# Eight masked copies of the messages per edge type, or seven and a difference weight

## The chip, the cores and the metric

The kernel runs on one core of one Trainium2 chip. The metric is the device time of one launch in microseconds (us), as the median of the runs.

## The reference, cut to what matters

Two layers of a relational graph network over 50,000 nodes and 50,000 edges, 128 features, 8 edge types. Each edge makes a message from its source row; the message is multiplied by the 128x128 weight of its type, divided by the number of edges of that type at its destination, and added up there.

```
m = jax.nn.relu(h[src] + xe)                     # one message an edge
seg = etype * n + dst
sums = jax.ops.segment_sum(m, seg, num_segments=R * n)
mean = sums / jnp.maximum(cnt, 1.0)[:, None]
out = jnp.einsum('rnd,rdo->no', mean.reshape(R, n, -1), w)   # R = 8 weights
out = out + h @ rt + b
h = _batch_norm(out, gamma, beta)                # then relu, in layer 0
```

Before layer 0 every row goes through a layer norm and relu, and at the end the input x is added.

## The kernel before

**Stages.** About 174 us of preparation (indices turned, edge counts, first 56 row gathers), then for each layer an edge loop and a node loop. The edge loop of layer 0 lies at about 174 to 1180 us of the span, its node loop at 1180 to 1525; the edge loop of layer 1 at 1524 to 2582, its node loop to 2825; then the output pass.

**Edge loop.** The edges are cut into tiles of 127 (one row is kept for a carried partial sum), 394 tiles a layer, four tiles a group (`H = 4`), so 99 groups a layer. A group is 128 partitions by 512 values. Its steps, each engine working through its own list in order:

- POOL (GpSimd) gathers four times 128 rows by index (line 468) 14 groups ahead and scatters four times 128 result rows (line 476) of the group itself. In the loop it issues them by turns: gather, scatter, gather, scatter (lines 507 to 512). The first scatter of a group waits for `ob_ready`, the first gather for the transposes of the group that held its buffer.
- DVE (VectorE) goes through this order (lines 736 to 747): layer-norm statistics of group i+3 (`group_stats`, layer 0 only), the masked copies of group i (`by_type`, line 719), scales of group i+3 (`group_scales`, layer 0 only, waits for ACT's square root), edge sum of group i+2 (`edge_sum`: line 703 in layer 0, lines 706, 707 and 709 in layer 1), and the matrix that joins equal destinations, of group i (`same_node`, line 732, waits for PE's `keys`).
- `by_type` makes eight copies of the messages `mt`, copy r being zero where the edge's type, read from PSUM, isn't r. It waits for PE to have finished the products two groups back (`mk` has two slots).
- PE (TensorE) multiplies, for each tile, the eight copies by the eight weights into one sum (`products`, line 1069), and then joins equal destinations (`node_sums`, line 1086). Transposes of group i+2 (`turn`, line 1039) stand behind the second tile's products of group i.
- ACT (ScalarE) writes `mt` (`message`, line 859), copies the products out (line 867), carries the last row from tile to tile (line 879) and copies the sums to `ob` (line 887), which has four slots and waits for the scatter that used the slot to land.

**Preparation's end.** PE turns the inverse counts (line 995), DVE copies them (lines 669 and 670) and goes straight into the loop. PE waits for all parameters (`params_in`, line 1031) before it. The weights of both layers lie in SBUF from the start (`w_sb`, loaded at line 832).

Of the kernel before, what the change touches and what calls it, by code (L numbers as in the profile page):

```python
# [6 lines left out]
P = 128  # L7
# [4 lines left out]
ALU = mybir.AluOpType  # L12
ACT = mybir.ActivationFunctionType
# [4 lines left out]
def wait(eng, sem, value):  # L18

    if value > 0:  # L20
        eng.wait_ge(sem, value)
# [20 lines left out]
def gnn_kernel(nc, x, src, dst, edge_attr, edge_type, weight, root, bias, gamma, beta, out):  # L42
    N, D = x.shape
    E = src.shape[0]
    L, R = weight.shape[0], weight.shape[1]
# [19 lines left out]
    W4 = H * D  # L65
# [16 lines left out]
    def tiles(g):  # L82
        return range(g * H, min(g * H + H, NT))

    ctx = ExitStack()
    with ctx:
# [3 lines left out]
        def sem(name):  # L90
            return ctx.enter_context(nc.semaphore(name))
# [14 lines left out]
        def part(which, mem, shape, dt=FP32):  # L106
            n = math.prod(shape[1:])
            flat = mem[:, used[which]:used[which] + n]
            used[which] += n
            if dt != FP32:  # L110
                flat = flat.bitcast(dt)
            if len(shape) == 3:
                flat = flat.rearrange("p (a b) -> p a b", a=shape[1])
            if len(shape) == 4:
                flat = flat.rearrange("p (a b c) -> p a b c", a=shape[1], b=shape[2])
            return flat

        def early(shape, dt=FP32):
            return part("arena", arena, shape, dt)
# [9 lines left out]
        w_sb = [early([P, R * D]) for l in range(L)]  # L129
# [65 lines left out]

        hb = early([P, HB, H, D])
        xb = early([P, XB, H, D])
        mt = early([P, 2, W4])

        rows_b = early([P, NB * P])[:, :].bitcast(BF16).rearrange("p (k b e) -> p k b e", k=2, b=NB)  # L200
        ident_b = early([P, P // 2])[:, :].bitcast(BF16)
        mk = mk_mem.rearrange("p (s r n) -> p s r n", s=2, r=R)
# [25 lines left out]
        def pb(name):  # L228
            return ctx.enter_context(nc.psum_tensor(name, [P, W4], FP32))

        ps_t = [pb("ps_t0"), pb("ps_t1")]
        ps_y = [pb("ps_y0"), pb("ps_y1")]
        ps_o = [pb("ps_o0"), pb("ps_o1")]
        ps_s = [pb("ps_s0"), pb("ps_s1")]
        ps_turn, ps_key, ps_type = ps_t[0], ps_t[1], ps_s
# [8 lines left out]
        params_in = sem("params_in")  # L244
# [25 lines left out]
        inv_out = sem("inv_out")  # L270
        tminv_in = sem("tminv_in")
        inv_ps = sem("inv_ps")
        got = [sem(f"got{s}") for s in range(HB)]
        xb_in = [sem(f"xb_in{s}") for s in range(XB)]
        scat_out = [sem(f"scat_out{s}") for s in range(OB)]
# [5 lines left out]
        m_ready = sem("m_ready")  # L281
        tr_ps = sem("tr_ps")
        mk_ready = sem("mk_ready")
        s_ready = sem("s_ready")
        y_ps = sem("y_ps")
# [246 lines left out]
        def _(dve):  # L532
            v = nc.vector
# [135 lines left out]
            own.link(v.tensor_copy(inv_t[:, :], ps_y[0][:, :]))  # L669
            own.link(v.memset(inv_t[0:1, :], 1.0))  # L670

            def flat(ap):
                return ap.rearrange("p c d -> p (c d)")

# [20 lines left out]
            def edge_sum(g, l):  # L695
                gg = l * NG + g
                w = len(tiles(g))
                h4 = hb[:, gg % HB, 0:w, :]
                x4 = xb[:, gg % XB, 0:w, :]
                if l == 0:  # L700
                    dve.wait_ge(h_ready, g + 1)
                    dve.wait_ge(xb_in[gg % XB], xb_count(gg))
                    v.tensor_tensor(flat(h4), flat(h4), flat(x4), ALU.add).then_inc(t_ready, 1)
                else:
                    dve.wait_ge(got[gg % HB], 16 * tiles_done(gg, HB))
                    own.link(v.tensor_tensor(h4, h4, bn_b[:, 0, :].unsqueeze(1).to_broadcast([P, w, D]), ALU.mult))
                    own.link(v.tensor_tensor(h4, h4, bn_b[:, 1, :].unsqueeze(1).to_broadcast([P, w, D]), ALU.add))
                    dve.wait_ge(xb_in[gg % XB], xb_count(gg))
                    v.scalar_tensor_tensor(flat(h4), flat(h4), 0.0, flat(x4), ALU.max, ALU.add).then_inc(t_ready, 1)

            def by_type(g, l):

                gg = l * NG + g
                n = len(tiles(g)) * D
                dve.wait_ge(types_ps, gg + 1)
                dve.wait_ge(m_ready, gg + 1)
                wait(dve, y_ps, gg - 1)
                for r in range(R):
                    ins = v.scalar_tensor_tensor(mk[:, gg % 2, r, 0:n], ps_type[gg % 2][:, 0:n], float(r), mt[:, gg % 2, 0:n],  # L719
                                                 ALU.is_equal, ALU.mult)  # L720
                ins.then_inc(mk_ready, 1)

# [13 lines left out]
            for l in range(L):  # L736
                for i in range(-3, NG):
                    if l == 0 and i + 3 < NG:
                        group_stats(i + 3)
                    if i >= 0:  # L740
                        by_type(i, l)
                    if l == 0 and i + 3 < NG:
                        group_scales(i + 3)
                    if 0 <= i + 2 < NG:
                        edge_sum(i + 2, l)
                    if i >= 0:
                        same_node(i, l)
# [18 lines left out]
                def add_own(c, l=l):  # L766
                    s = c % SLOTS
                    cc = l * NC + c
                    dve.wait_ge(ac_in[s], 16 * (l * chunk_uses(NC - 1 - (NC - 1 - s) % SLOTS) + chunk_uses(c)))
                    for q in range(2):  # L770
                        dve.wait_ge(own_ps, 2 * cc + q + 1)
                        rows = flat(ac[:, s, q * H:q * H + H, :])
                        v.tensor_tensor(rows, rows, ps_o[q][:, :], ALU.add).then_inc(sum_ready, 1)  # L773
# [47 lines left out]
        def _(act):  # L821
            a_ = nc.scalar
# [13 lines left out]
            n = (KEYS + P) // P  # L836
# [17 lines left out]
            def message(g, l):  # L854
                gg = l * NG + g
                n = len(tiles(g)) * D
                act.wait_ge(tr_ps, gg + 1)
                wait(act, mk_ready, gg - 1)
                a_.activation(mt[:, gg % 2, 0:n], ps_turn[:, 0:n], ACT.Relu).then_inc(m_ready, 1)  # L859

            def products_out(g, l):
                gg = l * NG + g
# [27 lines left out]
            for l in range(L):  # L890
                for i in range(-3, NG + 2):
                    if 0 <= i - 2:
                        carry(i - 2, 0, l)
                    if 0 <= i + 1 < NG:
                        message(i + 1, l)
                    if 0 <= i - 2:
                        carry(i - 2, 1, l)
                    if l == 0 and i + 3 < NG:
                        root_of(i + 3)
                    if 0 <= i - 2:  # L900
                        carry(i - 2, 2, l)
                    if 0 <= i - 1 < NG:
                        products_out(i - 1, l)
                    if 0 <= i - 2:
                        carry(i - 2, 3, l)
                        sums_out(i - 2, l)
                    if l == 0 and i + 3 < NG:
                        normalised(i + 3)
# [77 lines left out]
        def _(pe):  # L986
            te = nc.tensor

            def on_all(to, col):

                return te.matmul(to, col.to_broadcast([P, P]), ident[:, :], start=True, stop=True)
# [16 lines left out]
            for w in range(2):  # L1008
                te.matmul(ps_y[1][0:R, w * P:(w + 1) * P], tails[:, w, :], ident[:, :], start=True, stop=True)
                last = te.matmul(ps_y[1][0:R, (2 + w) * P:(3 + w) * P], through[:, w:w + 1].to_broadcast([P, R]), ident[:, :],  # L1010
                                 start=True, stop=True)
            last.then_inc(rows_ps, 1)
            pe.wait_ge(carries_ready, 1)
            for w in range(2):
                last = te.matmul(ps_s[1][:, w * R:(w + 1) * R], row_carry[:, w, w:w + P], ident[0:R, 0:R], start=True, stop=True)
# [14 lines left out]
            cols(ps_y[0], tm_inv).then_inc(inv_ps, 1)  # L1030
            pe.wait_ge(params_in, 16 * 5 * L)
            pe.wait_ge(meta_ready, 1)

            def turn(g, l):
                gg = l * NG + g
                pe.wait_ge(t_ready, gg + 1)
                wait(pe, m_ready, gg)
                for j in range(len(tiles(g))):
                    last = te.transpose(ps_turn[:, j * D:(j + 1) * D], hb[:, gg % HB, j, :], ident[:, :])  # L1039
                last.then_inc(tr_ps, 1)  # L1040
# [19 lines left out]
            def products(g, j, l):  # L1060
                gg = l * NG + g
                if j >= len(tiles(g)):
                    return
                c = slice(j * D, (j + 1) * D)
                if j == 0:
                    pe.wait_ge(mk_ready, gg + 1)
                    wait(pe, yb_ready, gg - 1)
                for r in range(R):
                    last = te.matmul(ps_y[gg % 2][:, c], mk[:, gg % 2, r, c], w_sb[l][:, r * D:(r + 1) * D],  # L1069
                                     start=r == 0, stop=r == R - 1)  # L1070
                if j == len(tiles(g)) - 1:
                    last.then_inc(y_ps, 1)

# [14 lines left out]
            for l in range(L):  # L1088
# [57 lines left out]
                if l == 0:  # L1146
                    pe.wait_ge(bn_ready, 1)
                    for k in range(2):
                        last = on_all(ps_o[0][:, k * D:(k + 1) * D], bn_col[:, 0, k:k + 1])
# [3 lines left out]
            for c in range(NC):  # L1153
                k = c - KEPT
                sums = kept[:, c, :] if k < 0 else spare[:, k % 2, :]
                for q in range(2):
                    pe.wait_ge(aff_ready, 2 * c + q + 1)
                    wait(pe, f_ready, 2 * (c - 1) + q + 1)
                    for j in range(H):
                        a = (q * H + j) * D  # L1160
                        last = te.transpose(ps_t[q][:, j * D:(j + 1) * D], sums[:, a:a + D], ident[:, :])  # L1161
# [24 lines left out]
```

## Time and profile before

| | us |
|---|---|
| median of 3 runs | 3026.44 |
| lowest and highest run | 2994.49, 3029.53 |
| profiled execution, its time | 3015.93 |
| its span, first to last instruction | 3014.1 |

The profile's page gives the busy time of each engine over the span, the span in 40 slices, and the chain of work that ended last. All instants below are us from the start of the span. An engine that is busy for most of the span need not set the end: one has to read, stage by stage, which wait ends last. "Issue" is time before an instruction in which its engine waited for nothing that the profile shows.

### The profile page before, as it was taken

To read this page: it belongs to the slowest core of one execution; us is meant where nothing else is said; L and a number is where in the kernel's file an instruction comes from. 1 tells how busy PE (TensorE), PEld (TensorE's weight loads), DVE (VectorE), ACT (ScalarE), POOL (GpSimd) and SP (SyncE) were. 2 spreads that over 40 slices of the span, in tenths; PEclk is the share of its full clock that TensorE was granted. 3 is DMA by queue.
4 is the path that set the end of the run, shared out by engine and by line. 5 is a ranking of instruction groups with operands and counts; after the bars stand their busy time and mean duration, and the time that the engine had idled before them with its cause. 6 is when DMAs were issued, how large, how long until landed. Compare 5 with 4: busy or idle time off the path is not lost.

```text
span 3014.1 us, 55442 instructions
## 1 busy us (share of the span) xinstructions
PE 2356.7 (78%) x20114; PEld 2261.9 (75%) x20114; DVE 2183.5 (72%) x5449; ACT 1088.4 (36%) x2709; POOL 1590.4 (53%) x1586
## 2 busy tenths in 40 slices
PE   0059999999888896767678888888988889787553
PEld 0059998888888896656678888888888889677443
DVE  2789988788878885777787777777777778365432
ACT  0024444343443443656622222222222222455443
POOL 5117777777777773000057777777777776100000
PEclk9999999999999998988889999999999999899755
DMA  9222232323222223666732122222222221567799
GB/s 371 80 91 94 85 100 87 101 94 103 92 92 97 70 62 88 231 224 224 240 113 57 55 58 61 62 65 68 68 66 67 68 69 43 185 240 270 261 318 310
DMA packets 224768, 386.65 MB, mean 128 GB/s; under 512 B 39743, under 2 KB 148046, under 8 KB 224492
## 3 DMA queue, kind: packets, MB, share of 16 engines
q1 hardware_dynamic: 149494, 214.88, 22.6%
q0 software_dynamic: 50432, 80.31, 8.8%
q10 hardware_dynamic: 24566, 87.86, 7.5%
q8 instruction: 164, 2.69, 0.4%
q14 instruction: 112, 0.92, 0.1%
HBM read 241.77 MB, written 164.19 MB: 135 GB/s over the span
## 4 chain that ended last, share of the span: by engine, by line
POOL 44%; PE 17%; issue 14%; DMA 13%; DVE 6%; another core or an unknown queue 2%; ACT 1%; SPq 1%; POOLq 1%; ACTq 0%; DVEq 0%
POOL acc L476 22%; POOL arena L468 22%; PE ps_y L1069 7%; DMA chunk_mem<-in_x_dram 5%; PE ps_o L1120 4%; DMA chunk_mem<-h_rows 4%; DMA out_dram<-chunk_mem 2%; PE ps_s L1134 2%; DMA spare<-spill 2%; DVE st L753 1%; PE ps_t L1110 1%; DVE chunk_mem L601 1%; PE ps_o L1086 1%; POOLq L476 1%
## 5 line engine op out<-in xcount | busy, mean ns | idle before, releaser
L1069 PE MATMUL ps_y<-arena 128*128 128x128 f32 x12608 | 1553.5, 277 | 7.9 <-DVE arena L719 7.9
L1069 PEld LDWEIGHTS ps_y<-arena 128*128 128x128 f32 x12608 | 1487.8, 194 | 8.4 <-DVE arena L719 8.4
L719 DVE SCALAR_TENSOR_TENSOR arena<-ps_s,arena 128x512 f32<-128x512 f32 x1584 | 960.4, 677 | 71.9 <-PE ps_y L1069 71.9
L476 POOL DMA_INDIRECT acc<-arena x788 | 810.6, 1029 | 296.6 <-issue 236.1
L468 POOL DMA_INDIRECT arena<-h_rows,arena x394 | 393.8, 1000 | 463.6 <-DMA h_rows<-chunk_mem 343.9
L468 POOL DMA_INDIRECT arena<-in_x_dram,arena x394 | 384.5, 976 | 229.8 <-issue 119.3
L1086 PE MATMUL ps_o<-arena 128*128 128x128 f32 x1576 | 332.0, 292 | 187.9 <-ACT arena L879 187.2
L732 DVE TENSOR_SCALAR arena<-ps_t,arena 128x128 f32<-128x128 f32 x788 | 269.1, 403 | 206.6 <-PE ps_t L1046 206.6
L1086 PEld LDWEIGHTS ps_o<-arena 128*128 128x128 f32 x1576 | 239.5, 192 | 222.5 <-ACT arena L879 221.2
L879 ACT ACTIVATE arena<-ps_o 1x128 f32<-1x128 f32 x786 | 205.3, 261 | 439.4 <-PE ps_o L1086 407.7
L887 ACT ACTIVATE arena<-ps_o 128x512 f32<-128x512 f32 x198 | 116.5, 589 | 508.6 <-DMA acc<-arena 506.0
L1120 PE MATMUL ps_o<-root_sb,ht 128*128 128x128 f32 x1568 | 228.3, 307 | 79.0 <-ACT ht L917 78.3
L1120 PEld LDWEIGHTS ps_o<-root_sb,ht 128*128 128x128 f32 x1568 | 213.8, 219 | 91.0 <-ACT ht L917 91.0
L867 ACT ACTIVATE arena<-ps_y 128x512 f32<-128x512 f32 x198 | 117.7, 595 | 302.4 <-PE ps_y L1069 300.9
L773 DVE TENSOR_TENSOR chunk_mem<-chunk_mem,ps_o 128x512 f32<-128x512 f32 x196 | 130.6, 685 | 88.9 <-PE ps_o L1120 81.5
L1110 PE MATMUL ps_t<-ident,chunk_mem 128*128 128x128 f32 x784 | 112.1, 289 | 92.3 <-DMA chunk_mem<-h_rows 52.2
L1110 PEld LDWEIGHTS ps_t<-ident,chunk_mem 128*128 128x128 f32 x784 | 90.3, 147 | 110.1 <-DMA chunk_mem<-h_rows 62.6
L851 ACT ACTIVATE arena<-arena,nmr,rstd 128x128 f32<-128x128 f32 x394 | 161.2, 481 | 6.0 <-DVE nmr L692 6.0
L927 ACT ACTIVATE chunk_mem<-chunk_mem,nmr,rstd 128x128 f32<-128x128 f32 x392 | 156.0, 482 | 10.6 <-DVE nmr L764 10.2
L859 ACT ACTIVATE arena<-ps_t 128x512 f32<-128x512 f32 x198 | 114.2, 577 | 108.3 <-PE ps_t L1039 107.7
L753 DVE BATCH_NORM_STATS2 st<-chunk_mem 128x6 f32<-128x128 f32 x392 | 80.5, 278 | 96.9 <-DMA chunk_mem<-in_x_dram 96.6
L818 DVE TENSOR_TENSOR chunk_mem<-chunk_mem,ps_t 128x512 f32<-128x512 f32 x98 | 65.1, 685 | 117.1 <-PE ps_t L1161 57.9
(135 smaller groups left out, 1882.9 us busy)
## 6 DMA issues: line engine op xcount, KB each, us to landing
chunk_mem<-acc SPq DMA_DIRECT2D x98, 512.0 KB, 4.1
arena<-in_edge_attr_dram SPq DMA_DIRECT2D x194, 256.0 KB
chunk_mem<-in_x_dram SPq DMA_DIRECT2D x98, 448.0 KB, 4.8
acc<-arena ACTq DMA_DIRECT2D x28, 896.0 KB, 26.3
acc<-arena SPq DMA_DIRECT2D x28, 896.0 KB
h_rows<-chunk_mem ACTq DMA_DIRECT2D x49, 512.0 KB, 4.1
chunk_mem<-h_rows SPq DMA_DIRECT2D x49, 512.0 KB, 4.7
out_dram<-chunk_mem ACTq DMA_DIRECT2D x49, 448.0 KB, 4.6
```

Source lines behind the costliest of these rows:

```text
L468: pool.indirect_dma_start(out=hb[:, gg % HB, t - g * H, :], out_offset=None, in_=(x, h1_tab)[l], in_offset=at(src_t[:, t:t + 1])).then_inc ...
L476: pool.indirect_dma_start(out=acc[l], out_offset=at(idx_t[:, t:t + 1]), in_=ob[:, gg % OB, t - g * H, :], in_offset=None, bounds_check=N - ...
L719: ins = v.scalar_tensor_tensor(mk[:, gg % 2, r, 0:n], ps_type[gg % 2][:, 0:n], float(r), mt[:, gg % 2, 0:n], ALU.is_equal, ALU.mult)
L732: ins = v.tensor_scalar(sm[:, gg % SM, c], ps_key[:, c], ikey_t[:, t:t + 1], inv_t[:, t:t + 1], ALU.is_equal, ALU.mult)
L773: v.tensor_tensor(rows, rows, ps_o[q][:, :], ALU.add).then_inc(sum_ready, 1)
L851: ins = a_.activation(row, row, ACT.Relu, scale=rstd[:, g % 2, j:j + 1], bias=nmr[:, g % 2, j:j + 1])
L879: a_.activation(yb[0:1, n % 2, (t + 1) % H, :], ps_o[gg % 2][0:1, j * D:(j + 1) * D], ACT.Copy).then_inc(carried, 1)
L927: ins = a_.activation(row, row, ACT.Relu, scale=rstd[:, c % 2, j:j + 1], bias=nmr[:, c % 2, j:j + 1])
L1069: last = te.matmul(ps_y[gg % 2][:, c], mk[:, gg % 2, r, c], w_sb[l][:, r * D:(r + 1) * D], start=r == 0, stop=r == R - 1)
L1086: te.matmul(ps_o[gg % 2][:, c], sm[:, gg % SM, c], yb[:, gg % 2, j, :], start=True, stop=True).then_inc(o_ps, 1)
L1110: last = te.transpose(ps_t[j // H][:, (j % H) * D:(j % H + 1) * D], xc[:, s, j, :], ident[:, :])
L1120: last = te.matmul(ps_o[q][:, j * D:(j + 1) * D], ht[:, c % 2, k:k + D], root_sb[:, l * D:(l + 1) * D], start=True, stop=True)
```

## The change

Instead of eight masked copies, seven are made (types 0 to 6). The eighth product of each tile multiplies the unmasked messages `mt` by the last type's weight, and the weights of the other seven types are replaced once, on DVE before the loop, by their difference to the last one. Since PE now reads `mt` itself, `mt` gets a third slot, and ACT waits before it writes a slot for the products of three groups back instead of for the masks of two groups back. PE waits once for the differences.

```diff
-        mt = early([P, 2, W4])
+        mt = early([P, 3, W4])
...
+            dve.wait_ge(params_in, 16 * 5 * L)
+            for l in range(L):
+                ws = w_sb[l][:, 0:(R - 1) * D].rearrange("p (r o) -> p r o", o=D)
+                ins = v.tensor_tensor(ws, ws, w_sb[l][:, (R - 1) * D:R * D].unsqueeze(1).to_broadcast([P, R - 1, D]), ALU.subtract)
+            ins.then_inc(w_ready, 1)
...
-                for r in range(R):
-                    ins = v.scalar_tensor_tensor(mk[:, gg % 2, r, 0:n], ps_type[gg % 2][:, 0:n], float(r), mt[:, gg % 2, 0:n],
+                for r in range(R - 1):
+                    ins = v.scalar_tensor_tensor(mk[:, gg % 2, r, 0:n], ps_type[gg % 2][:, 0:n], float(r), mt[:, gg % 3, 0:n],
                                                  ALU.is_equal, ALU.mult)
...
-                wait(act, mk_ready, gg - 1)
-                a_.activation(mt[:, gg % 2, 0:n], ps_turn[:, 0:n], ACT.Relu).then_inc(m_ready, 1)
+                wait(act, y_ps, gg - 2)
+                a_.activation(mt[:, gg % 3, 0:n], ps_turn[:, 0:n], ACT.Relu).then_inc(m_ready, 1)
...
             pe.wait_ge(meta_ready, 1)
+            pe.wait_ge(w_ready, 1)
...
-                for r in range(R):
-                    last = te.matmul(ps_y[gg % 2][:, c], mk[:, gg % 2, r, c], w_sb[l][:, r * D:(r + 1) * D],
-                                     start=r == 0, stop=r == R - 1)
+                for r in range(R - 1):
+                    te.matmul(ps_y[gg % 2][:, c], mk[:, gg % 2, r, c], w_sb[l][:, r * D:(r + 1) * D], start=r == 0, stop=False)
+                last = te.matmul(ps_y[gg % 2][:, c], mt[:, gg % 3, c], w_sb[l][:, (R - 1) * D:R * D], start=False, stop=True)
```

## Rows read from the trace of the kernel before

**Rows 1.** The page: busy time, share of span and instructions; then the chain by engine.
```profile
PE 2356.7 (78%) x20114; PEld 2261.9 (75%) x20114; DVE 2183.5 (72%) x5449; ACT 1088.4 (36%) x2709; POOL 1590.4 (53%) x1586
...
POOL 44%; PE 17%; issue 14%; DMA 13%; DVE 6%; another core or an unknown queue 2%; ACT 1%; SPq 1%; POOLq 1%; ACTq 0%; DVEq 0%
```

**Rows 2.** POOL's groups, 210 to 1085, then 1640 to 2490: busy, mean ns | idle before.
```profile
L476 POOL DMA_INDIRECT acc<-arena x335 | 341.9, 1021 | 129.2 <-issue 100.9 <-ACT arena L887 28.3
L468 POOL DMA_INDIRECT arena<-in_x_dram,arena x335 | 328.5, 981 | 102.2 <-issue 101.9 <-ACT arena L887 0.3
...
L476 POOL DMA_INDIRECT acc<-arena x321 | 335.8, 1046 | 97.8 <-issue 97.8
```

**Rows 3.** Lines 468 and 476, 210 to 1085, then 1600 to 2490: ns min/median/max.
```profile
L468 POOL DMA_INDIRECT arena<-in_x_dram,arena x335: 973/973/1450, 212.0 to 1084.1; - x168
...
L476 POOL DMA_INDIRECT acc<-arena x335: 1014/1014/1534, 210.7 to 1082.8; - x168
...
L468 POOL DMA_INDIRECT arena<-h_rows,arena x336: 969/973/1447, 1600.7 to 2489.4; - x168
...
L476 POOL DMA_INDIRECT acc<-arena x336: 1012/1012/1487, 1599.4 to 2488.0; - x168
```

**Rows 4.** Busy time in two stretches: us, PE, PEld, DVE, ACT, POOL, PEclk, DMA, GB/s.
```profile
210.00:1085.00 875.00, 804.29 (x7303) 788.19 (x7303) 735.41 (x2088) 366.74 (x1043) 670.28 (x670) 0.99 0.29 92
...
1600.00:2490.00 890.00, 778.06 (x7007) 756.86 (x7005) 685.96 (x1252) 217.06 (x581) 685.55 (x672) 0.99 0.21 63
```

**Rows 5.** The chain that ended last, in order of time: start, us, what.
```profile
1085.43 2.21 DMA acc<-arena
...
1101.82 1.79 PE ps_y L1069 x16
...
1110.80 1.79 PE ps_y L1069 x16
```

**Rows 6.** DVE's waits, 210 to 1085, then 1640 to 2490: total, times, longest.
```profile
DVE rstd L691 <- ACT sd L845: 76.1, 55, 2.7
DVE arena L732 <- PE ps_t L1046: 52.7, 85, 2.3
...
DVE arena L732 <- PE ps_t L1046: 127.5, 76, 4.3
DVE arena L719 <- PE ps_y L1069: 58.9, 80, 1.2
```

**Rows 7.** Timeline at the start of layer 0's edge loop: start, us, engine, line.
```profile
174.05 0.69 DVE L669 COPY arena<-ps_y 128x512 f32<-128x512 f32 x1 [5.87 <-PE ps_y L995]
...
184.65 4.87 DVE L719 SCALAR_TENSOR_TENSOR arena<-ps_s,arena 128x512 f32<-128x512 f32 x8
...
189.57 5.56 PE L1069 MATMUL ps_y<-arena 128*128 128x128 f32 x32 [4.64 <-DVE arena L719]
...
210.71 1.02 POOL L476 DMA_INDIRECT acc<-arena  x1 [27.40 <-ACT arena L887]
```

**Rows 8.** Two shapes of DVE's TENSOR_TENSOR: a timeline row, a group of lines.
```profile
159.86 0.57 DVE L625 TENSOR_TENSOR chunk_mem<-chunk_mem 128x392 f32<-128x392 f32 x1
...
L706 DVE TENSOR_TENSOR arena<-arena,bn_b 128x512 f32<-128x512 f32 x80 | 54.2, 678 | 0.0
```

**Rows 9.** Timeline of DVE, then of POOL, in layer 1's edge loop.
```profile
1710.29 4.87 DVE L719 SCALAR_TENSOR_TENSOR arena<-ps_s,arena 128x512 f32<-128x512 f32 x8 [1.07 <-PE ps_y L1069]
1715.08 0.68 DVE L706 TENSOR_TENSOR arena<-arena,bn_b 128x512 f32<-128x512 f32 x1
...
1716.52 0.69 DVE L709 SCALAR_TENSOR_TENSOR arena<-arena 128x512 f32<-128x512 f32 x1
...
1712.76 1.01 POOL L476 DMA_INDIRECT acc<-arena  x1 [0.30 <-issue]
...
1715.36 1.29 POOL L476 DMA_INDIRECT acc<-arena  x1 [0.30 <-issue]
1716.95 1.11 POOL L468 DMA_INDIRECT arena<-h_rows,arena  x1 [0.30 <-issue]
```

More of the change, by code:

```diff
@@ L272, in gnn_kernel @@
         inv_ps = sem("inv_ps")
+        w_ready = sem("w_ready")
         got = [sem(f"got{s}") for s in range(HB)]
```

## The prediction, made before the changed kernel was run

> **What bounds the kernel now.** Read the page's busy times first, and don't stop there [rows 1]: PE is busy 78% and DVE 72% of the span, POOL only 53%. By these numbers an eighth off DVE's largest group looks like a gain. But the chain that ended last runs 44% through POOL and 14% through "issue", and only 6% through DVE. The next view is therefore POOL's groups in the long stretch of each edge loop [rows 2]. From 210.7 to 1085 POOL issues 335 scatters and 335 gathers, and its idle time is 0.3 us before each (100.9 and 101.9 us of "issue"), beside 28.3 us of waits for ACT, nearly all of it one wait of 27.4 us that ended at 210.71 [rows 7]. A wait of 0.3 us that ends on nothing is the cost of handing over the next indirect DMA. So POOL is full, though the page calls it 77% busy there. By the medians [rows 3] a gather and a scatter take 0.973 + 1.014 us, with two hand-overs of 0.30 us 2.59 us, and a group of four pairs 10.38 us. Measured: (1085 - 210.7) / 335 x 4 = 10.44 us in layer 0, and (2490 - 1599.4) / 336 x 4 = 10.60 us in layer 1.
>
> PE needs less. When the last gather is issued the chain leaves POOL and goes through PE [rows 5]; there two like points of neighbouring groups lie 1110.80 - 1101.82 = 8.98 us apart. So PE has 1.4 us a group in hand in the POOL-paced stretches, and sets the pace only in the tails (about 1085 to 1168 and 2490 to 2568). DVE is busy 735.4 us of 875 and 686.0 of 890 [rows 4], 8.4 and 8.2 us a group, and where it stands idle it waits for ACT and PE [rows 6], which themselves are held by the four `ob` slots that POOL frees. In neither the paced stretch nor the tail does DVE end last.
>
> **The change part by part.**
>
> *One masked copy less.* L719 takes 4.87 us for eight copies [rows 7], 0.61 us each. 198 groups x 0.61 = 121 us of DVE's work go. In the paced stretches (85 groups a layer) this becomes longer waits for ACT and PE; it frees no PE time, since a tile still takes eight products of the same shape. If the cover were gone (POOL and PE faster than 8.4 us a group), it would be worth the 121 us. In the tails PE has no wait for DVE. Once it counts: at the start of layer 0, PE's first products wait for L719 until 189.57 [rows 7], and from there PE runs on to the first scatter at 210.71. That is -0.6 us. In layer 1 POOL starts its 56 gathers as soon as the node loop has ended and meets the first scatter when they are issued, so an earlier mask gains nothing.
>
> *The difference weights.* Two TENSOR_TENSOR of 128x896 at the head of DVE's loop, right behind the copy at 174.05 [rows 7]; behind them stand all statistics, scales and masks, and behind those PE and POOL's first scatter. The trace has 0.57 us for 392 elements and 0.68 us for 512 [rows 8], so 0.0009 us an element and about 1.0 us for 896 (an estimate), 2.0 us for both. Bounds: 0.68 us each (as 512), and 1.3 us each, two rows of 512. I take +2.0, between +1.4 and +2.6. PE had itself waited for the same parameters before the copy, so the new wait for them is over. PE's wait for the differences ends some 2 us into the prologue, before its first transposes, which need the edge sum anyway: nothing.
>
> *Third slot and new wait of ACT.* The new wait is for the products three groups back. `message` of a group waits first for its transposes, which stand on PE's list behind the second tile of the group two back, so the products of the group three back are always done when it passes. Cost nothing; the cover is that order. The old wait for the masks gives nothing back either: L859 waits for PE only.
>
> *Where DVE's work falls beside POOL.* This is the one place where DVE touches the bound. While L719 runs (1710.29 to 1715.16), the scatter at 1712.76 takes its usual 1.01 us [rows 9]. But the scatter at 1715.36 takes 1.29 us, and it starts inside L706 (1715.08 to 1715.76), which reads two SBUF tensors; the gather at 1716.95 takes 1.11 us and starts inside L709 (1716.52 to 1717.21). Both are late by (end of the DVE instruction - own start - 0.12): 0.40 - 0.12 = 0.28, 0.26 - 0.12 = 0.14. So POOL waits at its instruction's start for a two-input DVE instruction under way. Means against medians [rows 2, 3] give the present cost: 335 x (0.007 + 0.007) = 5 us in layer 0, where one such instruction a group exists (L703), and for the three a group of layer 1 (10.60 - 10.38) x 84 = 18 us. With seven copies L706 to L709 start 0.61 us earlier against the wait for PE that precedes L719 (80 waits in 80 groups [rows 6]). In layer 0, L703 stands behind a wait for ACT in 55 of 87 groups and stays there. What a shift does depends on where it lands: shifting the group shown, L706 to L709 cover 1714.47 to 1716.60, the scatter at 1715.36 falls into L707 and loses 0.40 us, the next start is free: 0.40 in place of 0.42. If instants were random, an instruction of 0.69 us in a POOL period of 1.30 us would be met 0.53 times and cost 0.3 us each time: 0.16 us a group in layer 0, 0.5 in layer 1. Against 0.06 and 0.22 now that is (0.10 + 0.28) x 85 = +32 us; if all meetings were missed, -23 us. I take +7 us, a quarter of the way to random, since most groups stay tied to ACT and PE as before.
>
> The Trainium skill, SBUF — State Buffer, section Who interferes with whom, states that DVE and GpSimd share one read and one write port, that a DVE instruction with at most one SBUF input outside the two-port modes doesn't contend, and infers that a tensor_tensor doesn't stall descriptor generation either. On L719 (one input in PSUM) the trace agrees, so taking one away frees POOL of nothing; on L706 the trace differs, with 0.28 us in the row. By the page's inference alone the +7 us would be 0.
>
> *Sum against the profiled execution's own 3015.9 us:* 3015.9 + 2.0 - 0.6 + 7 = 3024. The runs of before lie between 2994 and 3030 with the median 10 us above the profiled one. Three runs don't tell these two apart, so I give 3026.
>
> **The rivals.**
> 1. *DVE sets the pace after all* (a wait put down to ACT or PE is DVE's work in disguise): then the 121 us come off, 3016 - 121 + 1 = 2896. For it: DVE is busy 84% in layer 0's loop. Against: POOL's only idle there is the hand-over. A half of it isn't possible without POOL instructions getting shorter, and the medians equal the minima. Chance 0.03.
> 2. *Meetings at random or worse* (the other side): two-input instructions fall onto POOL's starts. At random 3016 + 1 + 32 = 3049. It decides the 2% (60 us) only from 0.35 us a group on, over all 170 paced groups; the most in layer 1 is two meetings of 0.57 us, 1.14 - 0.22 = +0.92 us x 85 = +78 us, 3095. For it: the groups are locked, so one bad position repeats. Against: a late POOL shifts itself out of it. Chance 0.14 for 3040 to 3075, 0.03 above.
> 3. *Meetings missed*: 3016 + 1 - 23 = 2994. Chance 0.09.
> 4. *PE becomes the bound through its clock.* The eighth product's operand is dense where a masked copy is mostly zeros. The granted clock is 0.99 of full in both paced stretches [rows 4], so nearly all at 2.4 GHz. For PE to pass 10.4 us a group from 8.98 us, some 27% of the time would have to be at 1.2 GHz; every further 10% costs about 0.6 us x 170 = 100 us. Nothing in the rows ties the clock to data. Chance 0.01.
>
> **How the numbers follow.** The forecast (POOL keeps the pace, meetings little changed) has 0.70 and its own range 3005 to 3045. Rivals 2 and 3 widen the range to 2992 to 3054, which leaves out rival 1, the worse half of rival 2, and 4. A measurement of this kernel tells about 2% (60 us) from no change. Faster by over 2%: rival 1, 0.03. Slower by over 2%: rival 4 and the top of rival 2, 0.04. Within 2%: 0.93.
>
> **What would show each step.** After the change: L719 x7 in about 4.26 us at the same 0.68 us each, DVE's busy time lower by about 120 us and its waits for ACT and PE longer by as much; POOL's idle before 468 and 476 still 0.30 us, its medians 0.973 and 1.014; the first scatter at 212.1 instead of 210.7; tail groups of 8.98 us; two 128x896 instructions near 175 us of about 1.0 us each. Means of 468 and 476 in layer 1 tell which way the meetings went. The forecast is wrong if POOL's median falls, if POOL shows waits for ACT in the paced stretch, or if the loops shorten by more than 25 us.

## The result

The changed kernel takes 3039.76 us in the median of 19 runs (3027.28 to 3056.18); the kernel before, run beside it, 3026.44 us (19 runs, 2994.49 to 3036.35). The ratio is 1.0048, with a 95% interval from 1.0033 to 1.0063: slower by half a per cent. In two later series on other occasions it was 1.0015 (0.9994 to 1.0037) and 1.0033 (1.0014 to 1.0053). The ratios are estimated over the runs of a series and need not equal the quotient of the two medians. The profiled execution took 3035.88 us, with a span of 3034.1 us.

The page of the changed kernel, its busy times and its chain by engine. Line numbers have moved: 476, 468, 719, 732, 703, 706, 707, 709 and 691 are now 477, 469, 726, 739, 710, 713, 714, 716 and 698. In the kernels of the experiments they lie a few lines off these.

```profile
PE 2361.3 (78%) x20114; PEld 2269.2 (75%) x20114; DVE 2069.5 (68%) x5253; ACT 1087.5 (36%) x2709; POOL 1586.2 (52%) x1586
...
POOL 44%; PE 17%; DMA 14%; issue 14%; DVE 5%; another core or an unknown queue 2%; ACT 1%; SPq 1%; POOLq 1%; ACTq 0%; DVEq 0%
```

DVE did lose what it was to lose: 2183.5 us [rows 1] became 2069.5, 114 us less. The chain is the same as before, 44% POOL and 14% hand-overs. The 114 us bought nothing.

They went into waits. DVE's waits in the long stretch of layer 0 (210 to 1085), then of layer 1 (1640 to 2490), to be held against [rows 6]:

```profile
DVE rstd L698 <- ACT sd L852: 125.8, 87, 3.2
...
DVE arena L739 <- PE ps_t L1054: 169.9, 79, 4.4
```

The wait for ACT grew from 76.1 to 125.8 us and now comes in all 87 groups; in layer 1 the wait before the joining matrix grew from 127.5 to 169.9 us. Each is about the 0.6 us a group that was taken out. POOL meanwhile is as full as it was; its scatters in layer 0, then its scatters and gathers in layer 1, in the same stretches (busy, mean ns | idle before):

```profile
L477 POOL DMA_INDIRECT acc<-arena x334 | 341.8, 1023 | 128.4 <-issue 100.9 <-ACT arena L894 27.6
...
L477 POOL DMA_INDIRECT acc<-arena x322 | 338.0, 1050 | 98.1 <-issue 98.1
L469 POOL DMA_INDIRECT arena<-h_rows,arena x322 | 317.0, 984 | 98.1 <-issue 97.2 <-PE ps_t L1047 0.9
```

The gathers of layer 1 in the kernel before, for comparison:

```profile
L468 POOL DMA_INDIRECT arena<-h_rows,arena x321 | 320.0, 997 | 97.8 <-issue 97.5 <-PE ps_t L1039 0.3
```

The hand-over is 0.30 us as in [rows 2]. The scatters' means rose by 2 and 4 ns, and that of layer 1's gathers fell by 13 ns.

**Where the 20 us between the two profiles lie, and why that is a trap.** The two spans differ by 20.0 us, more than the medians do (13.3). Cut at POOL's first and last scatter and gather of each layer, the traces give the following stretches in us. "Paced" runs from the first scatter of a layer to its last gather, "tail" from there to its last scatter, and "56 gathers" from layer 1's first gather to its first scatter. The last row is the excess: the sum of what POOL's durations exceed 0.973 us (gather) and 1.013 us (scatter) by in the two paced stretches, and 0.944 us in the 56 gathers. Three more profiles, which are told of below, stand beside the first pair.

| stretch | before | before, again | after | after, again | after, third |
|---|---|---|---|---|---|
| to the first scatter | 210.7 | 211.9 | 212.5 | 214.3 | 213.1 |
| paced, layer 0 | 878.6 | 878.1 | 879.6 | 880.1 | 880.1 |
| tail, layer 0 | 89.9 | 89.9 | 89.9 | 89.9 | 89.9 |
| node loop, layer 0 | 344.9 | 355.3 | 356.1 | 351.3 | 352.0 |
| 56 gathers, layer 1 | 75.2 | 74.4 | 73.5 | 73.0 | 74.4 |
| paced, layer 1 | 892.8 | 893.7 | 889.2 | 896.9 | 899.7 |
| tail, layer 1 | 88.2 | 88.2 | 88.4 | 88.1 | 88.1 |
| node loop 1 and output | 433.8 | 444.2 | 444.8 | 437.0 | 444.3 |
| excess of POOL's durations | 29.1 | 28.7 | 24.7 | 32.3 | 36.5 |

By the first pair of profiles alone, 22 us come from the node loops and the output pass, which the change doesn't touch; the preparation has lost 2 us and the edge loops have won 4. The second profile of the same kernel before takes this away: without any change, its node loop of layer 0 took 355.3 us and its last stretch 444.2. One row shows it, POOL's first gather of layer 1, which waits through the node loop; here in the changed kernel and then in the kernel before, profiled again (in brackets the idle time before it and what ended it):

```profile
1538.18 0.99 POOL L469 DMA_INDIRECT arena<-h_rows,arena  x1 [355.10 <-DMA h_rows<-chunk_mem]
```

```profile
1535.16 0.99 POOL L468 DMA_INDIRECT arena<-h_rows,arena  x1 [354.35 <-DMA h_rows<-chunk_mem]
```

So a difference of 10 us in a node loop or the output pass of one profile says nothing here; only medians of many executions, and stretches that repeat within 1 us (the paced and tail ones of the kernel before do), can carry an argument. In the changed kernel even the paced stretch of layer 1 doesn't repeat: 889.2, 896.9 and 899.7 us.

The excess accounts for this in full. Paced stretches and 56 gathers together take 1846.6 us in the first column, less the excess of 29.1 that is 1817.5; the other columns give 1817.5, 1817.6, 1817.7 and 1817.7. The nine further profiles of the experiments, with six to nine copies, cut edge sums or none, all give 1817.5 to 1817.7 as well. So in these stretches nothing but the length of POOL's indirect DMAs differs between any two of these kernels, and what a kernel gains or loses beyond its excess lies in the preparation or in the node loops and the output pass (the tails agree to 1 us).

### The profile page after: what moved, and what is told of

Its sections match the earlier page's. It is cut to its first block, busy times and chain, and to the rows that moved or that the text cites. A ratio compares the mean times of both kernels' runs of the same rounds, so it can differ in the third digit from the quotient of the medians.

```text
span 3034.1 us, 55245 instructions
## 1 busy us (share of the span) xinstructions
PE 2361.3 (78%) x20114; PEld 2269.2 (75%) x20114; DVE 2069.5 (68%) x5253; ACT 1087.5 (36%) x2709; POOL 1586.2 (52%) x1586
## 4 chain that ended last, share of the span: by engine, by line
POOL 44%; PE 17%; DMA 14%; issue 14%; DVE 5%; another core or an unknown queue 2%; ACT 1%; SPq 1%; POOLq 1%; ACTq 0%; DVEq 0%
POOL arena L469 22%; POOL acc L477 22%; PE ps_y L1077 7%; DMA chunk_mem<-in_x_dram 6%; PE ps_o L1128 5%; DMA chunk_mem<-h_rows 4%; DMA out_dram<-chunk_mem 2%; PE ps_s L1142 2%; DMA spare<-spill 2%; DVE st L760 1%; PE ps_t L1118 1%; DVE chunk_mem L602 1%; PE ps_o L1094 1%; PE ps_y L1078 1%
## 5 line engine op out<-in xcount | busy, mean ns | idle before, releaser
L1077 PE MATMUL ps_y<-arena 128*128 128x128 f32 x11032 | 1377.1, 277 | 6.7 <-DVE arena L726 6.7
L1077 PEld LDWEIGHTS ps_y<-arena 128*128 128x128 f32 x11032 | 1311.2, 194 | 7.2 <-DVE arena L726 7.2
L726 DVE SCALAR_TENSOR_TENSOR arena<-ps_s,arena 128x512 f32<-128x512 f32 x1386 | 843.3, 680 | 71.7 <-PE ps_y L1078 71.5
L1128 PE MATMUL ps_o<-root_sb,ht 128*128 128x128 f32 x1568 | 237.7, 315 | 89.9 <-ACT ht L924 89.9
L1078 PE MATMUL ps_y<-arena 128*128 128x128 f32 x1576 | 307.3, 277 | 0.0
L1128 PEld LDWEIGHTS ps_o<-root_sb,ht 128*128 128x128 f32 x1568 | 222.9, 227 | 101.7 <-ACT ht L924 101.7
L1078 PEld LDWEIGHTS ps_y<-arena 128*128 128x128 f32 x1576 | 242.0, 194 | 0.0
```

The source lines that it names most:

```text
L1078: last = te.matmul(ps_y[gg % 2][:, c], mt[:, gg % 3, c], w_sb[l][:, (R - 1) * D:R * D], start=False, stop=True)
L1128: last = te.matmul(ps_o[q][:, j * D:(j + 1) * D], ht[:, c % 2, k:k + D], root_sb[:, l * D:(l + 1) * D], start=True, stop=True)
```

## The experiments

**The two kernels once more, and two undone parts.** Theory A: the loss comes from where DVE's two-input instructions fall beside POOL's starts. Theory B: some other part of the change (difference weights, third slot, the product that reads `mt`) slows it. These four ran side by side, the kernel before at 3031.19 us.

The kernel before, unchanged:

> The kernel before, unchanged, to see how far its own stages vary between profiles. Theory A (the loss lies in the edge loops, where two-input DVE instructions meet POOL's starts): the node loops and the output pass vary by chance, so in this profile the stretch from the last scatter of layer 0 to the first gather of layer 1 may as well be near 356 us as near 345. Theory B (something of the change slows the node loops and the output pass by about 11 us each, although their code is unchanged): that stretch is near 345 us again and the stretch behind the last scatter near 434. Ratio to before 1.000 within 0.002 by both.

3029.01 us, ratio 0.9982 (0.9965 to 0.9998). This is the same kernel on both sides, and the interval doesn't reach 1: a difference of 0.2% is not a finding by itself. The node stretches are those of the table, 355.3 and 444.2 us. Theory B in the form that its own expectation gives is out.

The changed kernel, unchanged:

> The changed kernel once more. Both theories: ratio 1.005. Theory A: node-loop stretches drawn anew, 345 to 356 us and 434 to 445 us, with meetings in the edge loops of 20 to 30 us by sum. Theory B: again near 356 and 445 us.

3037.26 us, ratio 1.0015 (0.9994 to 1.0037), 8 us above the identical copy of before in the same series; excess 32.3 us. The loss is smaller than in the first series and smaller than the 1.005 that both theories expected, which the interval doesn't reach; the excess is a little over the expected 20 to 30 us.

The eighth copy made, but read by nobody:

```diff
-                for r in range(R - 1):
+                for r in range(R):
                     ins = v.scalar_tensor_tensor(mk[:, gg % 2, r, 0:n], ...
```

> The changed kernel with DVE still making the eighth masked copy, which nobody reads (the arithmetic of the result stays that of the change). DVE then has the timing of before. Theory A (where DVE's work falls beside POOL decides): ratio 1.0007, that is only the 2.1 us of the difference weights. Theory B (the rest of the change costs it): ratio 1.005 as with seven copies.

3027.19 us, ratio 0.9981 (0.9960 to 1.0002), excess 27.9 us, paced stretch of layer 1 892.7 us, as in the kernel before. Everything of the change is in this kernel but the missing instruction, and 10 us against the seven-copy kernel of the same series are gone (12 runs each; the two intervals touch only from 0.9994 to 1.0002). It is as fast as the identical copy of before, 0.9982, though theory A had expected 1.0007, just above its interval. So it is the taking away of a DVE instruction that costs, not the weights, the slot or the dense operand. Of the 10 us, the excess shows 4 (27.9 against 32.3 us, one profile each).

The subtractions moved ahead of a wait:

```diff
+            dve.wait_ge(params_in, 16 * 5 * L)
+            for l in range(L):
+                ...                              # the two subtractions
             dve.wait_ge(inv_ps, 1)
             own.link(v.tensor_copy(inv_t[:, :], ps_y[0][:, :]))
```

> The changed kernel with the two 128x896 subtractions moved ahead of DVE's wait for the turned inverse counts, where it stands idle for 5.7 us. Both theories: first scatter 2.1 us earlier, near 210.4 us, and 2 us less than the changed kernel in the median, if the later phases between DVE and POOL do not move; theory A allows a few us either way for moved meetings.

3037.31 us, ratio 1.0015 (0.9992 to 1.0037): no gain that can be seen in the median. The first scatter starts at 211.2 us, against the 210.4 expected, and 1.3 to 3.0 us earlier than in the three profiles with the late subtractions, so the prologue did shorten, as far as a preparation that itself varies by 2 us can tell; its 2 us are lost in the spread of the rest. This profile, of one of the slowest runs of this kernel (3050.65 us), is the one with the largest excess of all, 47.0 us, 37.1 of it in layer 1, whose paced stretch took 910.1 us. Its timeline shows the mechanism at its dearest, DVE first and POOL behind it:

```profile
2001.65 4.28 DVE L725 SCALAR_TENSOR_TENSOR arena<-ps_s,arena 128x512 f32<-128x512 f32 x7 [0.72 <-PE ps_y L1077]
2005.85 0.68 DVE L712 TENSOR_TENSOR arena<-arena,bn_b 128x512 f32<-128x512 f32 x1
...
2007.29 0.69 DVE L715 SCALAR_TENSOR_TENSOR arena<-arena 128x512 f32<-128x512 f32 x1
...
2016.86 0.68 DVE L712 TENSOR_TENSOR arena<-arena,bn_b 128x512 f32<-128x512 f32 x1
...
2004.87 1.01 POOL L477 DMA_INDIRECT acc<-arena  x1 [0.30 <-issue]
2006.18 1.19 POOL L469 DMA_INDIRECT arena<-h_rows,arena  x1 [0.30 <-issue]
2007.68 1.18 POOL L477 DMA_INDIRECT acc<-arena  x1 [0.30 <-issue]
...
2016.95 1.43 POOL L469 DMA_INDIRECT arena<-h_rows,arena  x1 [0.30 <-issue]
```

The gather at 2016.95 starts inside L712, which ends at 2017.54: 0.59 us less 0.12 is 0.47, and it is 0.46 us over 0.973. At 2006.18: 2006.53 - 2006.18 - 0.12 = 0.23, measured 0.22. The scatter at 2007.68 starts inside L715: 2007.98 - 2007.68 - 0.12 = 0.18, measured 0.17. The scatter at 2004.87 starts under the masks and takes its 1.01 us. The rule read from [rows 9] holds to 0.02 us.

It holds far beyond these rows. In the twelve profiles that have edge sums, between 210 and 1085 and between 1640 and 2490, 99 to 173 of some 1300 indirect DMAs are over 0.02 us longer than 0.973 (gather) or 1.013 us (scatter), 124 in the kernel before. Every one of them started while a DVE instruction with two SBUF inputs ran, and is longer by the time from its start to 0.12 us before the end of such an instruction, to 0.04 us. No DMA that started under the masks is over 0.02 us longer. The rule has one edge. With whole instructions of 0.69 us, a POOL start up to 0.03 us after the DVE instruction's is never lengthened, and one from 0.05 us to 0.08 us always is, by about 0.5 us. In the changed kernel the gather at 2275.33 starts 0.02 us into L713 and takes its 0.97 us, while L713 takes 0.75 us instead of 0.68.

**The cause taken away.** The edge sums are left out in both kernels, with all their waits kept. (One small DVE instruction with two SBUF inputs of 128x4 stays in layer 0; no POOL duration is longer for it in these two profiles.)

```diff
-                    v.tensor_tensor(flat(h4), flat(h4), flat(x4), ALU.add).then_inc(t_ready, 1)
+                    dve.sem_inc(t_ready, 1)
...
-                    own.link(v.tensor_tensor(h4, h4, bn_b[:, 0, :].unsqueeze(1).to_broadcast([P, w, D]), ALU.mult))
-                    own.link(v.tensor_tensor(h4, h4, bn_b[:, 1, :].unsqueeze(1).to_broadcast([P, w, D]), ALU.add))
                     dve.wait_ge(xb_in[gg % XB], xb_count(gg))
-                    v.scalar_tensor_tensor(flat(h4), flat(h4), 0.0, flat(x4), ALU.max, ALU.add).then_inc(t_ready, 1)
+                    dve.sem_inc(t_ready, 1)
```

> The kernel before without the edge sums of both layers (lines 703, 706, 707 and 709 left out, all waits kept): DVE then has no instruction with two SBUF inputs in the edge loops. Left out is adding the edge rows, and the normalisation of the gathered rows in layer 1. Theory A (POOL's starts wait for such instructions): POOL's durations fall to their medians in both loops, the excess over them from 5 + 4 + 20 us to below 2, and the whole falls by 27 to 30 us to a ratio of 0.990 to 0.991. Theory C (POOL's longer durations have another cause, such as DMA traffic): they stay, ratio 1.000.

> The changed kernel without the edge sums of both layers (same parts left out as in the eight-copy kernel without them). Theory A: the difference between seven and eight copies shrinks to the prologue's 1.5 us, so 0.9905 to 0.992. Theory B (something else of the change costs 10 us): 0.3% above the eight-copy kernel without edge sums.

3004.45 us, ratio 0.9919 (0.9897 to 0.9941), with eight copies; 3003.59 us, 0.9915 (0.9891 to 0.9939), with seven. The kernel before beside them took 3030.24. POOL's groups in layer 1, 1640 to 2460, with eight copies and then with seven (busy, mean ns | idle before):

```profile
L476 POOL DMA_INDIRECT acc<-arena x316 | 319.8, 1012 | 96.3 <-issue 96.3
L468 POOL DMA_INDIRECT arena<-h_rows,arena x317 | 308.4, 973 | 96.6 <-issue 96.6
```

```profile
L477 POOL DMA_INDIRECT acc<-arena x316 | 319.9, 1012 | 96.3 <-issue 96.3
L469 POOL DMA_INDIRECT arena<-h_rows,arena x316 | 308.3, 976 | 96.4 <-issue 96.4
```

The means are the medians of [rows 3], to 3 ns, and no duration is over 0.02 us longer: every long POOL duration was due to the edge sums. The excess is 1.0 and 3.2 us, and the paced stretch of layer 1 873.1 and 874.1 us in place of 892.8. The whole falls by 26 us, a little less than the 27 to 30 expected with eight copies, and about the excess of 29 us that the kernel before carries; this also shows that POOL alone sets the pace, since DVE has lost 2.1 us a group of layer 1 here and nothing but the excess is gained. Theory C is out. And the 10 us between seven and eight copies are no longer there (-0.9 us), though with 6 runs each a rest of up to some 8 us isn't excluded.

**The instant moved.** Nine copies (the two last unread, in a buffer with room for nine) and six:

```diff
-                for r in range(R - 1):
+                for r in range(R + 1):        # nine;   range(R - 2): six
```

> The changed kernel with DVE making nine copies, two of them read by nobody: the two-input instructions fall 0.61 us later than in the kernel before. Theory A: its time follows from where they fall beside POOL's starts; moved by 0.61 us out of the position of before, 3 to 15 us slower than the kernel before, ratio 1.001 to 1.005, all of it in POOL's durations. Theory D (only DVE's amount of work counts): slower too if the pace were DVE's, but then by 121 us against eight copies, 1.04.

> The changed kernel with six copies, the product of type 6 reading the copy of type 5 (so type 6 is summed wrongly; PE's work is unchanged). The two-input instructions fall 1.22 us earlier than in the kernel before, about one POOL period of 1.30 us. Theory A: nearly the position of before, one instruction on, so ratio 0.999 to 1.002. Theory D (less DVE work helps): 0.96. Theory B (something else of the change costs): 1.005 as with seven copies.

| copies | moved by, us | median, us | before beside it | ratio | excess, us |
|---|---|---|---|---|---|
| 6 | -1.22 | 3033.73 | 3030.24 | 1.0010 (0.9995 to 1.0025) | 31.7 |
| 7 | -0.61 | 3039.76, 3037.26, 3041.79 | 3026.44, 3031.19, 3029.5 | 1.0048, 1.0015, 1.0033 | 24.7, 32.3, 36.5 |
| 8 | 0 | 3027.19 | 3031.19 | 0.9981 (0.9960 to 1.0002) | 27.9 |
| 9 | +0.61 | 3047.84 | 3030.24 | 1.0063 (1.0038 to 1.0088) | 40.7 |

All of these have the difference weights, and each excess is that of one profile. The time doesn't follow the amount of DVE's work: six copies have 121 us of it less than seven and are no faster than eight, nine have 121 us more than eight and are the slowest, and no kernel lies more than 18 us off the kernel before beside it. Had the amount counted, nine against eight would be 1.04. The order of six, seven and eight is less certain, since most of their intervals overlap. Nine copies came out above the expected 1.001 to 1.005 by a hair, six within its range. The expectation had put all of the nine copies' loss into POOL's durations; of 18 us in the median the excess shows 12. That the loss is smallest near the old position fits theory A; no run sets the position by itself.

**A remedy, if theory A is right.** If POOL waits for the rest of a DVE instruction, shorter instructions must cost less. Each 128x512 instruction of the edge sums is cut into pieces by tile. The seven-copy kernels with pieces also make the difference weights early, as in the experiment above; the eight-copy one is the kernel before with nothing else changed.

```diff
-                    own.link(v.tensor_tensor(h4, h4, bn_b[:, 0, :].unsqueeze(1).to_broadcast([P, w, D]), ALU.mult))
...
+                    for k, how in ((0, ALU.mult), (1, ALU.add)):
+                        for j in range(0, w, 1):              # quarters;   range(0, w, 2), min(2, w - j): halves
+                            m = min(1, w - j)
+                            own.mark(v.tensor_tensor(h4[:, j:j + m, :], h4[:, j:j + m, :],
+                                                     bn_b[:, k, :].unsqueeze(1).to_broadcast([P, m, D]), how))
+                        own.join()
...
```

> Seven copies, the difference weights made early, and each two-input instruction of the edge sums cut into four of 128x128 (about 0.21 us each). Theory A: POOL waits at most for the rest of a short instruction, less 0.12 us, so the excess over the medians falls from 26 to 37 us over both edge loops to 3 to 8 us, and the ratio to the kernel before is 0.992 to 0.995, below both kernels; DVE gets about 0.7 us a group more in layer 1, still under POOL's 10.4. Theory E (any two-input instruction costs POOL the same whatever its length): four times the meetings, slower than seven copies.

> As seven_quarters, but cut into two of 128x256 (about 0.34 us each). Theory A: excess of 8 to 16 us, between the uncut and the quarters, ratio 0.994 to 0.998.

> The kernel before with only the edge sums cut into quarters. Theory A: the same gain as with seven copies, ratio 0.992 to 0.995, and the number of copies no longer matters within 0.1%, except for DVE's load of layer 1, 8.2 + 0.7 us a group, which stays under 10.4.

> The changed kernel once more, beside the cut ones. Ratio 1.002 to 1.005; the stretches of the node loops drawn anew (344 to 356 us and 434 to 445 us), the excess of POOL's durations over both edge loops 25 to 35 us.

| kernel | median, us | ratio to before (3029.5) | excess, us |
|---|---|---|---|
| seven copies, quarters | 3012.85 | 0.9945 (0.9926 to 0.9963) | 10.9 |
| seven copies, halves | 3016.10 | 0.9937 (0.9912 to 0.9962) | 21.3 |
| eight copies, quarters | 3006.13 | 0.9914 (0.9889 to 0.9938) | 10.9 |
| seven copies, uncut (third time) | 3041.79 | 1.0033 (1.0014 to 1.0053) | 36.5 |

The kernel with eight copies and quarters, 3006.13 us, has the lowest median of all that compute the whole result, below both original kernels. The pieces take DVE longer: in the seven-copy kernel with quarters the first eight pieces and the start of the third step lie 1702.44 - 1700.58 = 1.86 us apart,

```profile
1700.58 1.82 DVE L718 TENSOR_TENSOR arena<-arena,bn_b 128x128 f32<-128x128 f32 x8
1702.44 0.90 DVE L724 SCALAR_TENSOR_TENSOR arena<-arena 128x128 f32<-128x128 f32 x4
```

where it is 1716.52 - 1715.08 = 1.44 us with whole ones [rows 9]. DVE's work went up, and the kernel got faster, because POOL's mean durations in layer 1 fell, from 1046 and 997 ns in the kernel before to these with seven copies and quarters (1640 to 2470; with eight copies and quarters 1028 and 975):

```profile
L477 POOL DMA_INDIRECT acc<-arena x319 | 325.7, 1021 | 97.2 <-issue 97.2
L469 POOL DMA_INDIRECT arena<-h_rows,arena x318 | 311.1, 978 | 96.9 <-issue 96.9
```

The excess is larger than expected: 10.9 us in place of 3 to 8 with quarters, 21.3 in place of 8 to 16 with halves. Short pieces make each meeting cheaper, but hardly rarer: in the two long stretches 113 and 99 DMAs are over 0.02 us longer with quarters and 119 with halves, where the three profiles of the changed kernel have 115 to 139. The ratio came out as expected with seven copies and quarters, and just below what was expected with eight copies and quarters (0.992 to 0.995) and with halves (0.994 to 0.998). Theory E is out. Two things don't fit the expectation. Seven and eight copies with quarters were to be alike within 0.1% and are 0.3% apart, at equal excess; and halves are about as fast as quarters (3.3 us above in the median, 0.0008 below in the ratio), though their excess is twice as large. Both differences are within what the intervals allow, which overlap, and the second may be nothing but spread. The first stays open. By the stretches above it isn't in the edge loops. The repeated kernel came out within its expected ratio, its excess 1.5 us over the expected 35.

## Why the prediction was right and wrong

**What bounds the kernel: right.** POOL's hand-over was still 0.30 us, its medians were 1.012 to 1.014 and 0.973 us, the tails 89.9 and 88.4 us as before, and 114 us of DVE work went without a gain. With the edge sums left out, the time fell to POOL's own pace and no further. Rival 1 (DVE sets the pace after all) is out, by the change itself and by the kernel with nine copies.

**The prologue: right.** The two subtractions took 2.09 us against 2.0 forecast, and L726 4.28 us against 4.26. POOL's first scatter, forecast at 212.1 us, in the changed kernel (214.3 and 213.1 in its other two profiles, 2.0 us later in the mean than in the two of before, against 1.4 forecast):

```profile
175.73 2.09 DVE L676 TENSOR_TENSOR arena<-arena 128x896 f32<-128x896 f32 x2
...
212.58 1.02 POOL L477 DMA_INDIRECT acc<-arena  x1 [26.94 <-ACT arena L894]
```

**The new wait of ACT, the third slot, the dense operand: right, nothing.** The kernel with the eighth copy kept has all three and stands at 0.9981. Rival 4 (PE's clock) didn't come: the granted clock was 0.98 and 0.99 in the two paced stretches, against 0.99 and 0.99, so nearly all at 2.4 GHz.

**L703 stays where it is in layer 0: tied as forecast, not free of cost.** The forecast had 55 of 87 groups tied to ACT; with seven copies all 87 are. Its meetings still cost a little more: the excess of layer 0 is 6.0 to 6.6 us against 4.6 to 5.1.

**The meetings: right in kind, the size not settled.** The forecast said +7 us on the whole, a quarter of the way to random instants. Against 29.1 and 28.7 us, the three profiles of the changed kernel show an excess of 24.7, 32.3 and 36.5 us, a mean of 31.2, +2 us. With the 47.0 of the kernel with early weights, the mean is 35.1, +6 us. And the single profile that came with the result went the other way (-4 us); whoever has only that one would call the step false. That the sign was right is shown by the medians and the kernel with the eighth copy kept; the quarter was a guess. The random case was also priced too high by the forecast's own rule: a start at a random instant inside an instruction of 0.69 us, with 0.12 us free, costs 0.24 us in the mean and not 0.3, so random instants give 0.53 x 0.24 = 0.125 us an instruction, (0.065 + 0.155) x 85 = +19 us and not +32, and a quarter of it +5. The hand-worked example is right in its shape and not in its price: in the changed kernel, too, one of the three instructions is met a group, the second, but for 0.15 us here and not for 0.40. The scatter at 1717.21 starts inside L714, and no other start is met:

```profile
1716.79 0.69 DVE L714 TENSOR_TENSOR arena<-arena,bn_b 128x512 f32<-128x512 f32 x1
...
1717.21 1.16 POOL L477 DMA_INDIRECT acc<-arena  x1 [0.30 <-issue]
1718.67 0.97 POOL L469 DMA_INDIRECT arena<-h_rows,arena  x1 [0.31 <-issue]
```

0.27 us to the end of L714, less 0.12, is 0.15, and the scatter takes 1.16 us. What the forecast hadn't in view is how much the position drifts from one execution to the next: the changed kernel's excess varies by 12 us, and its runs by 24 to 29 us.

**The step that failed: the last line of the sum.** The terms gave +2.0 - 0.6 + 7 = +8.4 us on the profiled execution. The text then set the number at 3026, "three runs don't tell these two apart", and so dropped the 8.4 us: it forecast the median of the kernel before, 3026.44, to the microsecond, and with it no loss. Put onto that median the same sum is 3035, and the measured medians are 3037 to 3042, 6 to 13 us above the kernel before beside them. A difference that is worked out from one execution belongs on whatever base is chosen; the spread of the base doesn't cancel it. In the sum, the terms for the prologue (+1.4, measured +2.0) and for the meetings (+7, measured +2 or +6) both point the right way, and how close 3035 comes is in part luck, since the profiles find no more than 4 or 8 us of the loss in them. The measured time lies in the range (2992 to 3054), and the change is within 2%, but its sign was argued and then not forecast.

**What stays open.** The three series give +6, +12 and +13 us against the kernel before beside them. The prologue and the mean excess account for 4 of these, or 8 with the early-weights profile counted in. Whether the rest is spread or another effect of the missing instruction, these runs don't tell; nor do they say why seven copies with quarters are slower than eight with quarters. A rest can only lie in the preparation, the node loops and the output pass, or in the difference between the profiled executions and the median one. The node loop of layer 0 and the last stretch vary by 10 us each between the two profiles of the kernel before (343 to 356 and 434 to 445 over all profiles), which is more than what would have to be found there. What makes them vary is open too. The node loop's granted clock was 0.86 in the kernel before (345 us) and 0.85 in its second profile and in the changed kernel (355 and 356 us), so a mixture of 1.2 and 2.4 GHz in each, but which follows from which isn't shown.

## What to carry to other kernels

An engine that is busy for 53% of the span can be the bound of the longest stretches: look whether its idle time before each instruction there is only the hand-over. Work taken off another engine then buys nothing, and can cost, because it moves that engine's other instructions in time against the bound one; here the cheaper remedy was to make those instructions shorter, not fewer. And before reading a stage's difference out of two profiles, profile one of the kernels twice; here a sum of what the bound engine's instructions took too long explained every edge loop up to its tail to 0.2 us, where the raw spans misled.

## What the runs showed of the hardware

In these kernels, a POOL indirect DMA whose start falls into a DVE instruction with two SBUF inputs is longer by the rest of that instruction less 0.12 us: 0.46 us in the longest row shown, 0.5 us in the longest ones of the uncut kernels, and some 20 us in all over the edge loop of layer 1 in the kernel before. A DVE instruction with one input in SBUF and one in PSUM (the masks) never did this in any profile (1.01 us beside the masks). The Trainium skill, SBUF — State Buffer, section Who interferes with whom, has the rule for the second, and the trace agrees. For the first, the same section of the Trainium skill states that a DVE instruction with two SBUF inputs contends with a GpSimd instruction that reads SBUF, which fits what is measured here and which the prediction didn't weigh; it also infers that a tensor_tensor doesn't stall descriptor generation, and for these indirect DMAs the measurement differs and decides: without such instructions POOL's mean fell from 1046 to 1012 ns and the kernel by 26 us. What an indirect DMA reads at its start, no run shows.
